# A fused attention and feed-forward kernel: one row tile's bytes go to GpSimd, two context tiles' conversion to ScalarE, and one low part of W moves ahead of an output tile

## The reference, cut to what matters

```python
def fake_quant(x, scale, zp):              # scale 8/255, zp 128
    q = clip(round(x / scale + zp), 0, 255)
    return (q - zp) * scale

# x: (2, 1024, 2048), ctx_4096: (2, 2048, 2048)
x = x + matmul(fake_quant(layernorm(x)), fake_quant(ctx_4096))
# feed-forward part, on the tokens of layernorm(x)
probs = softmax(xf @ W_router.T); w = top-2 weights over 8 experts
h     = einsum('td,erd->ter', xf, lora_A)
x     = x + (xf @ W_base.T + b_base) + einsum('ter,eor,te->to', h, lora_B, w) * 2
```

## Time and profile before

| | |
|---|---|
| median of the timed runs | 992.72 us |
| the profiled execution, whole | 994.51 us |
| its span, first to last instruction | 992.7 us |
| PE busy | 961.9 us, 97% |
| DVE busy | 793.7 us, 80% |
| ACT busy | 431.2 us, 43% |
| POOL busy | 139.4 us, 14% |
| DMA | 185.66 MB |

### The profile page before, as it was taken

One profiled execution on the slowest core, in us unless ns is written; L12 is line 12 of the kernel. 1 busy time (PEld: TensorE's weight loads), 2 busy tenths in 40 slices (PEclk: granted clock), 3 DMA queues, 4 the chain that ended last, 5 costly groups with the idle time before them and its releaser, 6 DMA issues.

```text
span 992.7 us, 15032 instructions
## 1 busy us (share of the span) xinstructions
PE 961.9 (97%) x5813; PEld 523.3 (53%) x5813; DVE 793.7 (80%) x1469; ACT 431.2 (43%) x467; POOL 139.4 (14%) x176
## 2 busy tenths in 40 slices
PE   1899999999999999999999999999999999999998
PEld 1666666666699444444444444444444444444444
DVE  7988887989726876997885887857889788798885
ACT  4788877755632435464433453212232323322310
POOL 2635445573100000000000000000000000000000
PEclk9999999999999999999999999999999999999999
DMA  9967767787343337767665664268534143242220
GB/s 370 371 216 290 280 258 275 289 311 268 151 139 132 104 94 221 255 234 216 235 216 198 196 213 109 73 201 288 172 119 138 69 144 117 79 144 88 98 75 33
DMA packets 62312, 185.66 MB, mean 187 GB/s; under 512 B 6896, under 2 KB 19488, under 8 KB 56096
## 3 DMA queue, kind: packets, MB, share of 16 engines
q1 hardware_dynamic: 58648, 174.18, 49.4%
q0 software_dynamic: 1280, 2.12, 2.1%
q10 hardware_dynamic: 2312, 8.39, 2.1%
HBM read 151.07 MB, written 33.60 MB: 186 GB/s over the span
## 4 chain that ended last, share of the span: by engine, by line
PE 79%; DVE 4%; DMA 3%; issue 0%; ACT 0%; DVEq 0%
PE pair L1878 29%; PE pair L1854 27%; PE pair L1694 13%; PE pair L1816 5%; PE pair L1826 4%; DMA scratch<-w_max 1%; DMA spread<-scratch 1%; DVE w_p L1236 1%; PE pair L1890 1%; PE pair L1702 0%; ACT w_p L812 0%; DVE cent L1292 0%; DVE cent L1331 0%; DVE u L1401 0%; DVE u L1421 0%
## 5 line engine op out<-in xcount | busy, mean ns | idle before, releaser
L1854 PE MATMUL pair<-x2p,w_p 128*128 128x512 f16 x1536 | 337.0, 379 | 1.7 <-DVE w_p L1236 1.7
L1854 PEld LDWEIGHTS pair<-x2p,w_p 128*128 128x128 f16 x1536 | 150.1, 98 | 182.4 <-DVE w_p L1236 2.2
L1694 PE MATMUL pair<-q1T,ctx_q 128*128 128x342 f16 x1536 | 228.5, 309 | 4.1 <-DVE ctx_q L993 2.4
L1694 PEld LDWEIGHTS pair<-q1T,ctx_q 128*128 128x128 f16 x1536 | 148.2, 97 | 79.4 <-issue 2.9
L1878 PE MATMUL pair<-x2p,w_slot 128*128 128x512 f16 x744 | 163.8, 379 | 0.0
L828 ACT ACTIVATE sq<-pair,lsc 128x512 f32<-128x512 f32 x64 | 43.5, 681 | 207.5 <-PE pair L1826 171.6
L1619 POOL TENSOR_SCALAR ctx_u<-ctx_f,par 128x512 uint8<-128x512 f32 x128 | 113.8, 901 | 125.3 <-DMA ctx_f<-in_ctx 104.9
L1878 PEld LDWEIGHTS pair<-x2p,w_slot 128*128 128x128 f16 x744 | 72.7, 98 | 87.9
L856 ACT ACTIVATE w_slot<-w_q,usc 128x1024 f16<-128x1024 f32 x32 | 36.5, 1145 | 92.5 <-DVE usc L1452 27.2
L1878 PE MATMUL pair<-x2p,x2p 128*128 128x512 f16 x336 | 74.3, 379 | 0.0
L725 ACT ACTIVATE xt<-xt,colt 128x1024 f32<-128x1024 f32 x32 | 36.7, 1145 | 55.6 <-DVE xt L1008 55.6
(11 more groups left out here) (223 smaller groups left out, 1112.6 us busy)
## 6 DMA issues: line engine op xcount, KB each, us to landing
ctx_f<-in_ctx SPq DMA_DIRECT2D x32, 1024.0 KB, 7.5
xt<-in_xT SPq DMA_DIRECT2D x32, 512.0 KB, 4.8
w_r<-in_w_n SPq DMA_DIRECT2D x32, 512.0 KB, 7.5
w_f<-in_w_t SPq DMA_DIRECT2D x32, 512.0 KB, 5.9
w_q<-in_w_t SPq DMA_DIRECT2D x32, 512.0 KB, 5.0
outT<-u SPq DMA_DIRECT2D x63, 256.0 KB, 3.2
rows<-in_x SPq DMA_DIRECT2D x15, 1024.0 KB, 10.2
x_kept<-xt ACTq DMA_DIRECT2D x16, 512.0 KB, 5.2
```

The costliest lines, as they stand in the source:

```text
L1694: ins = M.matmul(bank[at % RING][:, 0:W3], ctx_q[n % NQ][:, k, :], q1T[b][:, k, c * W3:(c + 1) * W3], start=(k == 0), stop=(k == KT - 1))
L1854: M.matmul(base_bank(m)[:, :], w_p[j % 2][wh][:, k, :], x2p[0][:, k, xh, t], start=(k == 0 and q == 0), stop=(k == KT - 1 and q == 2))
```

## The change

Five hand-written orders or tables change.

1. Row tile 2 gets its bytes on POOL instead of ACT. POOL makes them behind context tile 0 and ahead of context tile 1.
2. Context tile 0 is converted on ACT instead of DVE. ACT now does both first tiles.
3. ACT's order: the square root of group 3 stands ahead of the copy of row tile 2, and the conversion of context tile 1 behind the bytes of row tile 3.
4. DVE's order: without the conversion of tile 0; `take_y(0, 0)` moves from in front of `ln_scale_of(4)` to behind the conversion of context tile 2. PE issues 8 extra matmuls instead of 24 behind chunk(0, 0).
5. The low part of W's fourth column tile (j + 1 = 3) is made before `plain_out(3)` instead of behind it.

```diff
-POOL_ROWS = [4, 6]
-POOL_AT = {1: 4, 2: 6}
+POOL_ROWS = [2, 4, 6]
+POOL_AT = {0: 2, 1: 4, 2: 6}
...
-ON_ACT = [1] + list(range(4, STEPS, 2))
+ON_ACT = [0, 1] + list(range(4, STEPS, 2))
...
             ln_copy(1)
-            ln_bytes_of(2)
+            ctx_act_of(0)
+            ln_std_of(3)
             ln_copy(2)
-            ln_std_of(3)
+            ln_bytes_of(3)
             ctx_act_of(1)
-            ln_bytes_of(3)
             ln_copy(3)
...
             ln_scale_of(2)
-            ctx_ready_of(0)
             ln_stats_of(3)
             ln_stats_of(4)
             ln_scale_of(3)
             ln_stats_of(5)
             ln_stats_of(6)
-            take_y(0, 0)
             ln_scale_of(4)
             ctx_ready_of(2)
+            take_y(0, 0)
             ln_stats_of(7)
...
+                if j == 2:
+                    w_low(j + 1)
                 plain_out(2 * j - 1)
-                if 1 < j and j + 1 < JT:
+                if 2 < j and j + 1 < JT:
                     w_low(j + 1)
...
             chunk(0, 0)
-            keep_busy(24)
+            keep_busy(8)
             turn(3)
```

## The result

The changed kernel took 993.89 us (median of 20 runs, 991.63 to 995.39), the kernel before 992.66 us (20 runs, 991.45 to 995.47). The ratio is 1.0013, with a 95% interval of 1.0007 to 1.0019. That is 1.2 us slower and less than 0.2%. It is outside the predicted range (989.1 to 992.4), and its sign is not the forecast's. Single runs of either kernel scatter by some 0.8 us, so an effect of 1 us shows in a median only.

The account below looks back on a forecast made before the run. PE, busy 97% of the span, bounds the kernel, so only its standstills or lower clock can be given back. Start -0.75 and low part -1.71 make -2.46 us from 992.72: 990.3 us, range 989.1 to 992.4.

Parts of the forecast that it names:

- What bounds the start: Start, up to PE's 1.11 us wait for DVE at 82.20: the kernel gains what DVE gains, not PE.
- DVE's 1.20 us, POOL's bytes, the square root of group 3: Start: DVE loses a conversion worth 1.20 us, POOL's row tile 2 bytes come out even, the root moves from 26.99 to 25.79.
- The pause of 1.25 us ahead of chunk(0, 0): PE at the start: row tile 2's later copy makes PE stand still some 1.25 us; chunk(0, 0) begins at 28.1.
- chunk(0, 0) took 2.78 us to its successor ...; I keep that: PE at the start: chunk(0, 0) keeps its earlier 2.78 us, part of it at the lower clock, ending at 30.9.
- The third rival: Start: the pause holds 1.2 GHz through chunk(0, 0), DVE 1.2 us late, total -0.5, 992.2 us; 8% for both forms.
- Its worse form: Start: the lower clock lasts over the transposes and chunk(1, 0) too; total +0.5 to +1.6, 993.8 us; half of 8%.
- The lower clock in chunk(2, 0) before: PE near 38 us: chunk(2, 0) at full clock takes 2.5 instead of 4.04 us, counted as nothing at the end.
- Rival 1: Start: POOL's port use holds DVE's copies, costing 0.5 to 1.1 of the first term; total 991.2 us; 25%.
- first term: Start of the kernel: DVE's statistics of row tile 7 come 0.75 us earlier, counted as -0.75 us.
- Second term: Before PE's tile 6 at 392.09: the 1.71 us wait for W's low part goes whole, -1.71 us.
- Rival 2: Before tile 6: the low part's wait isn't worth 1.71 us in timed runs, only the first term remains; 992.0 us; 12%.
- What the clock's rule would have said: PE's clock: the skill's rule lets the rate fall only after a pause over 2.45 us, so nothing would be slow.

Follow-up runs that it names:

- fill: The changed kernel with 28 instead of 16 extra matmuls ahead of chunk(0, 0), which fills the pause: ratio 0.9999 to the kernel before.
- fill_again: The changed kernel with 28 instead of 16 extra matmuls ahead of chunk(0, 0), repeated on another chip: ratio 1.0001 to the kernel before.
- head_only: The changed kernel without the move of W's low part, so only the new orders at the start: ratio 1.0014 to the kernel before.
- after_long: The changed kernel with 24 instead of 8 extra matmuls behind chunk(0, 0), the pause ahead of it left in: ratio 1.0008 to the kernel before.
- w_only: The kernel before with only the low part for j = 3 moved ahead of plain_out(3): ratio 0.9999 to the kernel before.
- copy_first: The changed kernel with ACT's copy of row tile 2 back ahead of the square root of group 3: ratio 1.0002 to the kernel before.
- pause_look: The kernel before with 4 instead of 16 extra matmuls ahead of chunk(0, 0) and 8 instead of 24 behind, profiled again: ratio 1.0022.

## Why the prediction was wrong, step by step

- **What bounds the start: right up to 82 us, not beyond.** PE waits for DVE at 82 us in both kernels, and of the 1.19 us that DVE lost at the start 0.57 arrived there. The forecast carried DVE's shift to the end of the kernel without a loss, and that step failed too. In fill DVE has nearly the gain that was forecast, and PE still has it at this wait (it resumes at 81.48, 61.96 us behind the scale of row tile 2, against 62.99 and 62.53 in the two traces of the kernel before). At the end of the first stage it is gone (253.48 us in fill and 252.42 in fill_again behind that scale, against 253.15 and 252.49), and the time is that of the kernel before.
- **DVE's 1.20 us, POOL's bytes, the square root of group 3: right.** Forecast 25.79 for the root, measured 25.95; turn 2 at 23.80 against 23.68 before.
- **The pause of 1.25 us ahead of chunk(0, 0): right** (1.28; chunk at 28.25, forecast 28.1).
- **"chunk(0, 0) took 2.78 us to its successor ...; I keep that": the step that failed.** It took 4.51 (28.25 to 32.76), by itself 4.72 and 4.72 in two traces, 4.15 in head_only, 3.88 in after_long; with the pause filled 2.48 to 3.06 in five traces. That is 1.7 us on the way to turn 3. The eight extra matmuls took 0.63 instead of 0.5. From 31.4 for turn 3 this gives 33.4, the measured 33.39; ACT's copy, its root and DVE's scale follow by the list. The forecast treated as constant a duration that already mixed both rates, after adding just in front of it what the same text had seen lower the clock at 38 us.
- **The third rival had this mechanism**, with +1.2 us at DVE against a measured 1.19 (1.04 by the head's distance), turn 3 at 33.4 and the root at 36.2 against 35.91. It got a chance of 8%, half of it for this form, whose total of 992.2 us was still too low since it took off the same 1.71. Its sign, a clock row of 0.50 between 28 and 35 us, did not appear: the row says 1.00 while the chunk is slow. Its worse form didn't come: chunk(1, 0) and chunk(2, 0) took 2.49 and 2.50 us.
- **The lower clock in chunk(2, 0) before**: it is gone (2.50 against 4.04), and the forecast that this is worth nothing at the end fits what was measured. The kernels with the pause in the old order have it too (2.50 us) and are the slowest. And of 117 timed runs of the kernel before, in four sets, 31 have a mean granted clock of 1.000 and the others less, as in the traces in which chunk(2, 0) is slow (0.998); the medians of the 31 lie 0.5 us above, 0.5 above, 0.5 below and 0.5 below the others of their set.
- **Rival 1, the held copies: they came, and cost little.** Two copies of 0.76 and 0.77 us, as it said. But in the filled kernels, which have them too, the head's distance is 0.64 to 0.71 us less than before, so of the forecast 0.75 they take some 0.1 and not 0.5 to 1.1. Its own sum is also off: 0.5 to 1.1 less of the first term leaves a total of -1.4 to -2.0, not -1.3 to -1.7.
- **Second term, -1.71: the mechanism right, the size wrong.** The low part ran at 386.31 and tile 6 didn't wait:

```profile
386.31 2.47 DVE L1235 SCALAR_TENSOR_TENSOR w_p<-w_f,wsc,w_p 128x1024 f16<-128x1024 f32 x2
```

  But the wait was in one trace of eight, its mean over all traces some 0.4 us, and the move alone measures 0.9999. Rival 2 (12%) comes near this. Forecast and rival 2 leaned on the same number, the 1.79 us between the median and the profiled execution: that gap was in good part the very wait that was then subtracted a second time (994.51 - 1.71 = 992.8, close to the median of 992.72; the second trace of the kernel before, without the wait, took 992.19).
- **The sum with the measured terms**: the start +1.19, of which +0.57 reaches 82 us, plus what the row loads add (PE +2.16 at 142 us in this trace, +1.88 at the end of the stage), second term about -0.4: +1.5 where the runs say +1.2. The +1.88 is from one pair of traces and includes loads whose landing scatters.
- **What the clock's rule would have said.** The Trainium skill (TensorE: Matmul & The Clock Gate, Why this matters for your kernels) lets the rate fall only after a pause longer than either here. At 38 us the kernel before contradicts it: the granted clock fell in a pause of 2.45 us. On the pause ahead of chunk(0, 0) it doesn't bear, since no rate fell there: it had not risen yet. The eight matmuls of turn 2 took 1.03 us ahead of the pause, those of turn 3 0.61 behind the chunk. The prediction read "nothing falls" as "nothing would be slow", and left a rise that comes later to the third rival; filling the pause changed the chunk by 2.24 us.

**Open.** Why 16 fewer extra matmuls behind chunk(0, 0) cost the kernel before 1.1 us in two measurements, and the pause 1.0 us more, with nothing of either visible on DVE at the start. That the row loads' landing carries it is suggested by the waits (4.6 and 4.2 us), but the changed order with the pause filled has waits of 4.3 and 3.8 and w_only has 4.1, both without a loss. So by which way the changed kernel's 1.2 us reach the end is open as well. And copy_first's 3.97 us chunk without a pause.

## What to carry to other kernels

When a change opens a pause in TensorE's list shortly after it has begun to work, price the work behind it at both rates, and look at what waits for that work in order; filling the pause with matmuls that nobody reads gave the loss back here (0.9999 and 1.0001), though not measurably where 24 matmuls followed the chunk. Compare the starts of two traces from an instruction behind the first loads, not from the start of the span: the loads moved everything by up to 1.2 us. A wait that stands in one profiled execution and hangs on a trip through DRAM is not yet a wait of the kernel: look at a second trace before subtracting it, above all when that execution is longer than the median by about the same amount. And a gain of a microsecond early in a load-fed stage must be followed to the next waits for loads, where it can vanish.

## What the runs showed of the hardware

The record of the granted clock is not to be trusted in the first 33 us here. Stretches of PE in the changed kernel (length, busy and instructions, granted clock, DMA share, GB/s), answering to the earlier trace rows:

```profile
24.50:27.90 3.40, 2.47 (x36) 1.00 1.01 419
27.90:31.30 3.40, 3.05 (x11) 1.00 1.00 412
```

The second says 1.00, but the 16 matmuls of 342 columns that fill it and the time behind it took 4.51 us to their successor, 282 ns each, and the same 16 at 39.01 took 2.34, 146 ns each. That is about half of the rate, so the level was 1.2 and not 2.4 GHz. The duration of a known instruction tells the rate, the clock column alone does not. The stretch ahead had 2.47 us of work in 3.40; fill has all of it filled:

```profile
24.50:27.90 3.40, 3.40 (x47) 1.00 1.01 422
```

The moment at which the rate rises also varies by itself: chunk(0, 0) took 2.95 to 3.26 us in six traces with the same list ahead of it in the old order, and 3.88 to 4.72 in four with the pause in the new one. And the length of a pause alone doesn't decide whether the rate falls. In the kernel before PE waits 2.45 us ahead of chunk(2, 0), the granted clock is 0.50 and the chunk takes 4.04 us. In pause_look it waits as long at the same place:

```profile
38.63 2.50 PE L1694 MATMUL pair<-q1T,ctx_q 128*128 128x342 f16 x16 [2.45 <-DVE ctx_q L993]
```
```profile
38.10:41.50 3.40, 2.87 (x28) 1.00 1.02 422
```

GpSimd's four pieces took 4.00 us beside DVE's conversion and 3.04 otherwise. Trips of the same small tensor through DRAM ended 0.7 to 3.8 us behind the same PE instruction over the traces. This scatter of 3.1 us is more than the 2.46 us that the forecast had for the whole change.
